# A four-layer graph network on one core: attention in rotated tile order, and data handed over on chip between the stages

## The reference, cut to what matters

```python
x = _layernorm(x + L0(x, edge_index))   # attention by q.k, 4 heads, skip product, output product, norm
x = _layernorm(x + L1(x, edge_index))   # attention by leaky_relu(al_src + al_dst), 4 heads, norm, gelu MLP, norm
x = _layernorm(x + L2(x, edge_index))   # two sums of relu(x[src]) over the edges, each with a two-layer MLP
x = _layernorm(x + L3(x, edge_index))   # a sum with degree norms, then attention with one head
```

## Time and profile before

| | us |
|---|---|
| median of 3 runs (3879.44 to 3882.41) | 3881.09 |
| the profiled execution | 3878.65 |
| its span | 3876.9 |
| TensorE busy | 3705.8 (96%) |
| VectorE busy | 2282.5 (59%) |
| ScalarE busy | 2042.2 (53%) |
| GpSimd busy | 534.9 (14%) |

### The profile page before, as it was taken

How to read it: one execution, slowest core, us unless ns; L and a number is a source line. 1 busy time by engine, 2 the same in 40 slices (tenths; PEclk the granted TensorE clock), 3 DMA queues, 4 the chain that set the end, 5 groups by cost and what they waited for, 6 DMA issues and landing times. The chain is left out here.

```text
span 3876.9 us, 69921 instructions
## 1 busy us (share of the span) xinstructions
PE 3705.8 (96%) x27529; PEld 2886.1 (74%) x27530; DVE 2282.5 (59%) x4502; ACT 2042.2 (53%) x3736; POOL 534.9 (14%) x599
## 2 busy tenths in 40 slices
PE   6999969999999999699999999799999999999999
PEld 3666647677777676587777777688888888888887
DVE  8999936555655655499999999600012221005665
ACT  3555546666666666499999999600001110003554
POOL 1000000111111111100005667500000000000000
PEclk9999979999999999899999999999999999999999
DMA  2555572332333233533343333154343333334332
GB/s 95 226 229 210 237 243 85 110 112 91 114 99 104 91 115 104 145 132 116 120 173 104 113 113 111 60 211 147 129 145 138 138 137 126 136 120 144 138 138 72
DMA packets 177941, 520.61 MB, mean 134 GB/s; under 512 B 54385, under 2 KB 142454, under 8 KB 144502
## 3 DMA queue, kind: packets, MB, share of 16 engines
q1 hardware_dynamic: 175110, 509.49, 37.8%
q10 hardware_dynamic: 2544, 7.08, 0.6%
HBM read 354.22 MB, written 162.29 MB: 133 GB/s over the span
## 5 line engine op out<-in xcount | busy, mean ns | idle before, releaser
L1858 PE MATMUL t_acc<-t_r,t_ct 128*128 128x256 f32 (+1 forms) x3750 | 856.0, 380 | 20.0 <-DMA t_r<-d_r 16.2
L1036 ACT ACTIVATE a_sm<-a_p_t 128x1024 f32<-128x1024 f32 (+1 forms) x800 | 669.4, 837 | 372.9 <-PE a_p_t L974 356.6
L1858 PEld LDWEIGHTS t_acc<-t_r,t_ct 128*128 128x128 f32 x3750 | 701.4, 190 | 114.1 <-DMA t_r<-d_r 16.6
L974 PE MATMUL a_p_t<-ident,a_sm 128*128 128x128 f32 x5000 | 702.8, 280 | 36.6 <-ACT a_sm L1036 20.2
L1030 ACT ACTIVATE a_sm<-a_sm,a_negm 128x1024 f32<-128x1024 f32 (+2 forms) x600 | 703.1, 1172 | 43.1 <-DVE a_negm L1098 42.8
L974 PEld LDWEIGHTS a_p_t<-ident,a_sm 128*128 128x128 f32 x5000 | 562.5, 143 | 212.9 <-issue 194.1
L988 PE MATMUL a_p_o<-a_sm,a_v 128*64 128x128 f32 x10000 | 700.6, 279 | 10.2 <-ACT a_sumT L1043 9.1
L988 PEld LDWEIGHTS a_p_o<-a_sm,a_v 128*64 128x64 f32 x10000 | 555.8, 137 | 188.1 <-issue 109.9
L1118 DVE CUSTOM_DVE_ANT_0 a_sm<-a_p_s,sh_rows 128x400 f32<-128x400 f32 x800 | 427.2, 571 | 426.8 <-PE a_p_s L960 415.2
L960 PE MATMUL a_p_s<-sh_a_bc,a_q 64*128 64x400 f32 x1600 | 397.8, 557 | 27.7 <-DMA sh_rows<-d_logs 21.7
L1139 DVE SCALAR_TENSOR_TENSOR a_sm<-sh_a_bc,sh_al 128x3125 f32<-128x3125 f32 x100 | 346.2, 3462 | 15.0 <-PEq L52 11.6
(11 more groups left out here) (248 smaller groups left out, 3682.2 us busy)
## 6 DMA issues: line engine op xcount, KB each, us to landing
t_ct<-d_ct SPq DMA_DIRECT2D x74, 1600.0 KB, 6.6
sh_rows<-d_full SPq DMA_DIRECT2D x50, 1600.0 KB, 7.1
d_logs<-logs SPq DMA_DIRECT2D x25, 1664.0 KB, 7.0
sh_rows<-d_logs SPq DMA_DIRECT2D x25, 1664.0 KB
d_ct<-ct SPq DMA_DIRECT2D x25, 1600.0 KB, 5.3
d_full<-sh_rows SPq DMA_DIRECT2D x25, 1600.0 KB, 6.3
t_ct<-d_full SPq DMA_DIRECT2D x25, 1600.0 KB, 6.8
t_x<-d_x SPq DMA_DIRECT2D x75, 128.0 KB, 6.6
```

The costliest lines, as they stand in the source:

```text
L974: m = nc.tensor.transpose(p_t[u % 2][:, i * P:(i + 1) * P], sm[buf][:, a * P:(a + 1) * P], ident[:, :])
L1036: nc.scalar.activation(sm[buf][:, a_row[u] * P:a_row[u + 1] * P], p_t[u % 2][:, 0:turns[u] * P], ACT.Copy).then_inc(s_copy, 1)
L1858: m = self.nc.tensor.matmul(self.acc[t % 2][:, 0:width], self.ct[t % 3][:, a * P:(a + 1) * P], rows[:, a, 0:width], start=a == 0, stop=a = ...
```

## The change

- `Shared` is made before the counting stage. One wide buffer holds in turn the edge tables and the counts, then the keys, the source terms, and at last the messages, the third row of counts and the last attention's weights.
- The first attention takes the tiles in the order 23, 24, 0, 1, ... 22 (`tile_at`). The rows of logarithms of tiles 23 and 24 are neither stored nor loaded; VectorE masks row 23 at the end of the counting stage.
- SyncE loads the keys of tiles 0 to 22 and the first queries in the last tile of the counting stage and the keys of the last two tiles at its end; the next stage waits for them by semaphores that both stages share.
- In the hand-over between the attentions the source terms of the last two tiles are stored later, in tiles 2 and 3 of the next stage.
- The second norm's gain and bias move from GpSimd to VectorE, as two instructions with two tensor operands.
- At the end of the second attention SyncE loads the first three rows of counts and the first 20 tiles of messages into buffers that the sums use; ScalarE writes the last five tiles of messages there itself. The end no longer waits for the stores.

```diff
+def tile_at(j):
+    return (j + NT - 2) % NT
+KEPT = 20
+MESSAGES = NT * (D + 1)
...
 class Shared:
-        self.a_bc = sb("a_bc", [P, 2, 2, NPAD])
+        wide = sb("wide", [P, MESSAGES + 2 * NPAD])
+        self.a_bc = wide[:, 0:4 * NPAD].rearrange("p (h k n) -> p h k n", h=2, k=2)
+        self.messages = wide[:, 0:MESSAGES].rearrange("p (a n) -> p a n", a=NT)
+        self.row2 = wide[:, MESSAGES:MESSAGES + NPAD]
+        self.weights = wide[:, MESSAGES + NPAD:MESSAGES + 2 * NPAD]
+        self.q = [sb(f"q{i}", [P, H0, P]) for i in range(2)]
+        self.counts = [wide[:, i * NPAD:(i + 1) * NPAD].rearrange("p (a d) -> p a d", a=NT) for i in range(2)]
+        self.kt = wide[:, 2 * NPAD:4 * NPAD].rearrange("p (h n) -> p h n", h=H0)
...
 def build_counts
+                def hand_keys(a, b):
+                    proj.stored_keys(sp, b)
+                    for h in range(H0):
+                        rows = w_kt[(h % 2) * HD:(h % 2 + 1) * HD, h // 2, :, :].rearrange("p j n -> p (j n)")
+                        for r in range(2):
+                            lo, hi = max(a * P, r * HALF_K), min(b * P, (r + 1) * HALF_K)
+                            if lo < hi:
+                                sp.dma_start(shared.kt[r * HD:(r + 1) * HD, h, lo - r * HALF_K:hi - r * HALF_K], rows[:, lo:hi]).then_inc(shared.s_kt, 16)
...
+                    if last:
+                        hand_keys(0, NT - 2)
+                        proj.stored_keys(sp, NT - 1)
+                        hand_queries()
                     wait_alone(sp, s_group_out, (j + 1) * GPT)
...
-                store_logs(NT - 2, 1)
                 proj.store_vs(sp, NT - 1)
-                store_logs(NT - 1, 0)
+                hand_keys(NT - 2, NT)
...
+                dve.wait_ge(s_tbank_out, (NT - 1) * NTU)
+                for e in range(NFULL):
+                    c = slice(e * ROW // NFULL, (e + 1) * ROW // NFULL)
+                    v.scalar_tensor_tensor(logs[1][:, c], logs[1][:, c], STEEP, logs[1][:, c], ALU.mult, ALU.min).then_inc(shared.s_full, 1)
...
 def attend
-                    if not (isinstance(j, int) and j < 2):
-                        wait_alone(sp, s_kept[par], half * 32)
-                    sp.dma_start(full[par][:, :], row(log_dram, j)).then_inc(s_in[par], 16)
+                    if j >= 2:
+                        sp.wait_ge(s_kept[par], half * 32)
+                        sp.dma_start(full[par][:, :], row(log_dram, tile_at(j))).then_inc(s_in[par], 16)
...
-                        sp.wait_ge(s_in[0], 16 * n_in)
...
-                    P_.store(sp, NT - 2, 1, (NT - 2) // 2)
+                    P_.store_rows(sp, NT - 2, 1, (NT - 2) // 2)
+                    P_.store_values(sp, NT - 2, 1, (NT - 2) // 2)
                     P_.store_rows(sp, NT - 1, 0, (NT - 1) // 2)
...
+                    if p == 0 and j in (2, 3):
+                        i = 3 - j
+                        c = tile_at(NT - 1 - i)
+                        sp.dma_start(al_src_dram[:, :, c * P:(c + 1) * P].rearrange("h k p -> p (h k)"), shared.as_[i][:, :], allow_slow_non_contiguous=True).then_inc(shared.s_terms[i], 16)
...
-                P_.stored(sp)
+                    if j == NT:
+                        units = passes * NT * heads
+                        sp.wait_ge(s_mask, units - heads)
+                        sp.dma_start(shared.rows[0][:, 0:NPAD], row(ct_dram, 0)).then_inc(shared.s_sum[0], 16)
+                        sp.wait_ge(s_lift, units)
+                        for i in range(2):
+                            sp.wait_ge(shared.s_x2[i], rows_stored(KEPT - 2 + i))
+                        sp.dma_start(shared.messages[:, 0:KEPT, :], r2_dram[:, 0:KEPT, :]).then_inc(shared.s_messages, 16)
+                        sp.wait_ge(s_mask, units)
+                        sp.dma_start(shared.rows[1][:, 0:NPAD], row(ct_dram, 1)).then_inc(shared.s_sum[1], 16)
+                        sp.dma_start(shared.row2, row(ct_dram, 2)).then_inc(shared.s_sum[2], 16)
...
-                    for h in range(heads):
-                        if h == 1:
-                            act.wait_ge(s_in[0], 16 * n_in)
-                        for r in range(2):
-                            act.dma_start(kt[r * HD:(r + 1) * HD, h, :],
...
-                    for e in range(NFULL):
-                        mask_logs(0, 0, 0, e)
...
 post_a1, dve
                 if (lag, s) == (4, 0):
+                    dve.wait_ge(DL.sem, DL.at(jj, "aggr2"))
+                    v.scalar_tensor_tensor(t[:, :], t[:, :], n2.mv[:, 0:1], rows["g2"][:, :], ALU.subtract, ALU.mult).then_inc(DL.sem, 1)
+                    dve.wait_ge(DL.sem, DL.at(jj, "gain2"))
                     dve.wait_ge(PL.sem, PL.at(jj, "rstd2"))
-                    v.tensor_scalar(z[:, :], t[:, :], n2.mv[:, 0:1], n2.rs[:, 0:1], ALU.subtract, ALU.mult).then_inc(DL.sem, 1)
+                    v.scalar_tensor_tensor(z[:, :], t[:, :], n2.rs[:, 0:1], rows["be2"][:, :], ALU.mult, ALU.add).then_inc(DL.sem, 1)
...
 post_a1, pool
-                    pool.tensor_tensor(z[:, :], z[:, :], rows["g2"][:, :], ALU.mult).then_inc(PL.sem, 1)
-                    pool.wait_ge(PL.sem, PL.at(jj, "g2"))
-                    pool.tensor_tensor(z[:, :], z[:, :], rows["be2"][:, :], ALU.add).then_inc(PL.sem, 1)
-                    pool.wait_ge(PL.sem, PL.at(jj, "be2"))
...
 post_a1, act
+                    to = r2[tp] if jj < KEPT else messages[:, jj, :]
...
 Tail
-        self.r = [sb("r0", [P, NT, D + 1]), sb("r1", [P, NT, D])]
-        self.ct = [sb(f"ct{i}", [P, NPAD]) for i in range(3)]
+        self.r = [shared.messages, sb("r1", [P, NT, D])]
+        self.ct = [shared.rows[0][:, 0:NPAD], shared.rows[1][:, 0:NPAD], shared.row2]
...
-        for i in range(NT // PIECE):
-            a = i * PIECE
-            sp.dma_start(self.ct[0][:, a * P:(a + PIECE) * P], self.ct_dram[0, :, a * P:(a + PIECE) * P]).then_inc(self.s_first[i], 16)
-            sp.dma_start(self.r[0][:, a:a + PIECE, :], self.r2[:, a:a + PIECE, :]).then_inc(self.s_first[i], 16)
         load_x(0)
         gin_weights(0)
-        load_row(1)
-        load_row(2)
```

More of the change, by code:

```diff
@@ L252, in build_counts @@
         zeros = sb("zeros", [1, GW], BF16)
-        ct = [sb(f"ct{i}", [P, NT, P], FP32) for i in range(2)]
-        logs = [sb(f"logs{i}", [P, ROW], FP32) for i in range(2)]
+        ct, logs = shared.counts, shared.rows
         ct_own = sb("ct_own", [P, P], FP32)
@@ L702, in attend @@
         if dot:
-            full = shared.rows
-            kt = shared.a_bc[:, 1, :, :].rearrange("p k n -> p (k n)").rearrange("p (h n) -> p h n", h=heads)
-            q = [sb(f"q{i}", [P, heads, P]) for i in range(2)]
+            full = [shared.rows[1], shared.rows[0]]
+            kt, q = shared.kt, shared.q
             p_s = [pb(f"p_s{i}", [P, UNIT]) for i in range(2)]
         else:
-            mask = [shared.rows[1], shared.rows[0]]
+            mask = shared.rows
             a_bc, al = shared.a_bc, shared.al
@@ L713, in attend @@
         s_v = sem("values")
-        s_k = [sem(f"keys{h}") for h in range(heads)]
         s_src = [sem(f"source_terms{h}") for h in range(heads)]
@@ L1100, in mask_logs @@
                 def mask_logs(j, par, half, e):
-                    if e == 0:
-                        wait_alone(dve, s_in[par], (half + 1) * 16 * n_in)
+                    if e == 0 and j >= 2:
+                        dve.wait_ge(s_in[par], loaded(j))
                     c = slice(e * ROW // NFULL, (e + 1) * ROW // NFULL)
@@ L1500, in make @@
         zT = sb("zT", [P, 4, P])
-        x2 = [sb(f"x2{i}", [P, D]) for i in range(2)]
+        x2, messages, s_lift = shared.x2, shared.messages, scores
         r2 = [sb(f"r2{i}", [P, D + 1]) for i in range(2)]
@@ L1509, in make @@
         s_tin = [sem(f"post_in{i}") for i in range(2)]
-        s_out = [sem(f"post_stored{i}") for i in range(2)]
+        s_out = shared.s_x2
         s_init = sem("post_init")
@@ L1786, in load_x @@
                 sp.wait_ge(self.DO.sem, self.DO.at(i - 2 * NT - 2, "relu"))
+            if t == KEPT:
+                for k in range(2):
+                    sp.wait_ge(self.shared.s_x2[k], rows_stored(NT - 1 - k))
             if t == SUMS:
@@ L2099, in masked @@
         if k == 0:
[L2100 removed]
+            dve.wait_ge(self.s_ct[t % 3], 16 * (t // 3))
         dve.wait_ge(self.s_lift, n + 1)
```

216 lines of the change are left out of this document (121 added, 95 removed).

## The result

The changed kernel takes 3858.18 us (median of 4 runs, 3855.42 to 3861.59), the kernel before in the same comparison 3881.75 (3879.44 to 3884.26): ratio 0.9938, interval 0.9922 to 0.9954. The change is worth 23 to 24 us, not 44, and 3858 lies above the range of 3828 to 3852. The profiled executions say the same: 3855.42 us (span 3853.6) against 3878.65.

A forecast was written before the change was run, and what follows sets the result against it. TensorE's matmuls were taken to bound the last 1350 us, with barriers closing earlier stages. Terms 20.2 + 4.6 + 4.4 + 14.6 = 43.8 us off 3881.1 gave 3837 us; own range 3830 to 3844, full range 3828 to 3852.

The forecast's parts named there:

- Place 1: End of counting stage, start of first attention: early key and query loads start the first masking at 504.9, gaining 20.2 us.
- the data travel beside counting work that no engine waits for them in: Last counting tile: early key and query loads, 8.5 us at 372 GB/s, fit where DMA engines stand mostly at 0.
- Rival A: Start of first attention: keys come late, queued loads holding stores back; gain there only 10.6 us, time 3846.9; chance 0.14.
- no row at the start: Start of first attention: no row is loaded or masked, since VectorE masks row 23 in the counting stage.
- one score takes 0.85 us, so the first masking: Start of first attention: first score at about 504.1, one score of 0.85 us, so first masking at 504.9.
- place 3: Second pass of second attention: gain and bias on VectorE save net 0.19 us a tile over 23 tiles, 4.4 us.
- From there the pipeline fills in an order that the change leaves alone: First attention after its first masking: the rotated order moves no work, cost 0.
- Place 2: Seam between the attentions: source-term stores moved into the next stage leave ScalarE last, gaining 4.6 us.
- Rivals B and C: Second pass: B, VectorE loses 0.55 us a tile, 3855.7, chance 0.11; C, GpSimd held back, slower, 3936, chance 0.04.
- Place 4: End of second attention and first tiles of the sums: no awaited stores, prefetched rows and messages, gaining 14.6 us.
- Row wait and low clock: First tiles of the sums: second tile's 3.77 us wait for its row goes, and 1.9 us of low clock after it.
- Rival D: Start of the sums: the hand-over is not ready, so 8.6 us stay; time 3846, chance 0.09.

The follow-up runs named there:

- Experiment 2: Changed kernel with the eight key loads of the first 23 tiles issued one tile earlier: 3855.61 us, ratio 0.9939.
- experiment 3: Changed kernel without loading queries and rows of logarithms for tiles 2 to 24 of the first attention: 3841.28 us, ratio 0.9899.
- experiment 6: Kernel before, run again: 3881.87 us; kernel before without the query loads of tiles 2 to 24: 3886.87 us, ratio 1.0013.
- experiment 8: Changed kernel without query loads (3841.94 us), one edit each: keys a tile earlier 3837.01; place 2 undone 3846.20; place 3 undone 3848.28; place 4 hand-over undone 3857.09.
- experiment 7: Changed kernel with gain and bias of the second norm moved back from VectorE to GpSimd: 3862.88 us, ratio 0.9958.

## Why the prediction was wrong

Of 43.8 us 23.5 came, by the two profiles (the same group of products in the sums starts at 2522.57 and stood at 2546.05).

**Place 1, forecast 20.2, measured 11.7: wrong.** The first masking at 513.41 is past 510, one of the prediction's own signs of being wrong. The step that failed is "the data travel beside counting work that no engine waits for them in": 8.5 us at 372 GB/s, and the key store's 5.2 us of landing taken over from the earlier trace rows, where only stores of the same tile stood ahead of it. What was true of the issues was not true of the data. The 372 GB/s were read from loads over all 128 partitions; these loads write 64 partitions each, and the engines moved 230 GB/s at a share of 1.02. At that rate the 2.9 MB take some 13 us, and the store came behind them. Why these loads moved more slowly is not shown. The empty stretch was misread too: the earlier trace rows has 0 from 486.5 to 494.0, not 488.5 to 496, and from there on the engines are full; 8.5 us of data would not have fitted into those 7.5 us either. Rival A named this outcome (10.6 us, "SyncE's queue holds the counts and key stores back behind 3.2 MB") and got 0.14 of the chance, because I held the empty slices of the earlier trace rows against it: they say that there is room in the time, not that the store would be first. Experiment 2 takes the key loads away from in front of the store, and the first masking starts at 505.0. The issues and "no row at the start" stood; "one score takes 0.85 us, so the first masking" did not: it starts 1.86 us behind the first score, also in experiment 2, where a start 0.9 us sooner made up for it. The 16 of place 1 and the 9 and 2 of place 3 in the forecast's own range stand there without a working.

**Not a step at all, forecast 0, measured -10.4: wrong.** "From there the pipeline fills in an order that the change leaves alone" was taken as "and takes the same time". The order is the same, but the first attention has 15 to 17 us of stops now and 5 to 8 before. All but some 3 us of them go without the loads of queries and rows (experiment 3), so they hang on transfers inside the tile and not on engine work alone. Why the changed kernel has more of them stays open. Slow instruction pages do not account for it (experiment 6), nor do the queries by themselves, since the kernel before has stops of 14.3 us without them. The trace of before had the sign of it: tiles of 42.2 us beside some of 43 to 44. I looked at the seams and at the second pass, and not at this stretch, which is more than a quarter of the time.

**Place 2, forecast 4.6, measured 4.9 (4.3 by experiment 8): right.** With the store of source terms moved, the block follows ScalarE after 0.9 us. The prediction's 1.2 us for the barrier were 1.3 by the earlier trace rows less 0.1 for the wake-up, which was my estimate.

**Place 3, forecast 4.4, measured 3.9 (4.1 by experiment 8, 3.3 by experiment 7): right in mechanism, 0.5 off in size.** The half residual fell from 0.62 to 0.29 us and ScalarE's wait from 0.6 to 0.4 a tile; the long masking stayed at 3.8. What stood beside the residual before was GpSimd's addition of the bias, L1630. It lay beside the masking, ended at 2415.14, 0.47 us into the half residual, and took 3.78 us, against 0.72 in the last tile, where nothing was masked:

```profile
2411.36 3.78 POOL L1630 TENSOR_TENSOR a_z<-a_z,a_be 128x256 f32<-128x256 f32 x1
...
2509.38 0.72 POOL L1630 TENSOR_TENSOR a_z<-a_z,a_be 128x256 f32<-128x256 f32 x1
```

The norm's wait for GpSimd is 0.53 us behind the new instruction, where it was 0.77 without it: the new instruction's 0.48 us lay in that wait but for the 0.15 us by which the norm starts later behind the lift. GpSimd's power took 0.66 us beside the new instruction and 0.57 in experiment 8 with place 3 undone, so 0.09 more where the prediction added 0.08:

```profile
2399.80 0.66 POOL L1606 TENSOR_TENSOR a_n_rs<-a_n_ve,a_half_pow 128x1 f32<-128x1 f32 x1
```

```profile
2392.16 0.57 POOL L1606 TENSOR_TENSOR a_n_rs<-a_n_ve,a_half_pow 128x1 f32<-128x1 f32 x1
```

Rivals B and C fall.

**Place 4, forecast 14.6, measured 13.4: right, two sizes off.** ScalarE's last copy came 1.1 us sooner of its own (1.7 forecast; 0.9 in experiment 8), the block follows it 2.6 us sooner (2.4), the first product 4.9 (4.8). Row wait and low clock, 3.8 and 1.9, came to 4.8 together: the wait went, but the first tile itself now starts right behind the block in the low clock (granted 0.50 to 2508.2 us) and takes 14.79 us for its 56 products. The prediction's figures in GHz are in no trace: the profile gives the clock as a share, 0.50 at 2540 us and 1.00 from 2546.05 to 2558.89 in the kernel before, and the forecast's 1.9 us rest on these two and on the times of the earlier trace rows. The 0.2 us left between the block and the first product were my estimate; 0.20 was measured. Rival D falls.

**The sum of the misses** is 8.5 + 10.4 + 0.5 + 1.2 - 0.3 = 20.3 us. With the keys a tile earlier and without query loads the time is 3837.01 us, the number forecast, by chance and in a kernel that leaves work out; the best that computes everything took 3842.99.

## What to carry to other kernels

An empty stretch on the DMA engines hid these loads, but not from what was issued behind them: the key store landed after 12.6 us behind them and after 5.2 without them. Before filling such a stretch, time the data by the rate of loads of the same shape, and ask which store lands behind them. When a suspect is seen at one stop, look for it in the tiles that do not stop: the slow pages were there too. When a change moves only the edges of a stage, still compare the tile times within it, before and after; a stage that TensorE fills to 99% lost 10 us here to stops of up to 3 us each, which the page's groups show only as a little more idle time. And when run times scatter by 10 us, find a variant in which they do not, and weigh the parts on that.

## What the hardware showed that I had not expected

- Loads of 64 partitions moved at 230 GB/s with all engines busy, in this case at 62% of the 372 GB/s of the earlier trace rows.
- The scatter of the run times (12 us for the changed kernel) went with the stops: without the loads of queries it was 2 us in four kernels and 5 in a fifth. The slow runs were not profiled, so that they have more stops is inferred; and in the kernel before without these loads it was 8 us.
- Instruction pages of 16 KB that took 3.1 to 3.8 us, against the 0.9 of a quiet stretch, went by without a stop of the tile (9 and 12 in the changed kernel) or with at most 0.8 us of one (eight tiles of experiment 3's kernel).
- Packets of 13 KB took 0.55 us in one place and 2.9 us in another, with a quarter of the engines' time idle in the slow one. Ahead of the slow one the store of source terms had been issued (1113.99 us, 4.4 ahead of the row load); from then to 1120 us 1248 of the 1641 packets were under 512 bytes. Whether it is the cause was not tried.
- 64 products of one column, ahead of anything else and at a granted clock of 0.50, took 27.5 us, 0.21 us for each of the 128 records.
